# Products that nothing reads, put in front of TensorE's waits in the short stages of the last batch

## The reference

```python
# layer 2, feed-forward ("s5"): activations rounded to 8 bits, ternary weights
h = silu(bit_linear(x, w_gate)) * bit_linear(x, w_up)        # 256 -> 1024
h = rms_norm(h, ln_weight)
x = x + tanh(g) * bit_linear(h, w_down)                      # 1024 -> 256
# layer 3, cross part ("s6"), n = layernorm(x)
attention = softmax((ctx @ Wq.T + bq) @ (ctx @ Wk.T + bk).T)
x = x + tanh(g) * einsum('bln,bmn->blm', n, attention)
# layer 3, feed-forward ("s7"): ternary weights, 256 -> 2048 -> 1024 -> 256
h = silu(gate) * up
x = x + tanh(g) * rms_norm(h) @ wq_p.T
```

## Time and profile before

| what | us |
|---|---|
| median of 3 runs | 1062.55 |
| the profiled execution: its own time | 1062.66 |
| its span in the trace | 1060.9 |
| PE busy (share of the span) | 860.6 (81%) |
| DVE busy | 713.6 (67%) |
| ACT busy | 557.3 (53%) |
| POOL busy | 276.0 (26%) |

### The profile page before, as it was taken

How to read it: one execution, slowest core, us unless ns; L and a number is a source line. 1 busy time by engine, 2 the same in 40 slices (tenths; PEclk the granted TensorE clock), 3 DMA queues, 4 the chain that set the end, 5 groups by cost and what they waited for, 6 DMA issues and landing times.

```text
span 1060.9 us, 13344 instructions
## 1 busy us (share of the span) xinstructions
PE 860.6 (81%) x4116; PEld 616.7 (58%) x4120; DVE 713.6 (67%) x1716; ACT 557.3 (53%) x1318; POOL 276.0 (26%) x365
## 2 busy tenths in 40 slices
PE   3779988755898987798979789979998779699355
PEld 1435655534566865655757567558776656476134
DVE  3896789774548768976889866765568772244643
ACT  8887874222464654446535555653466534466313
POOL 1100212102244201630763113415310423200205
PEclk9999999977999999889999999989999979699568
DMA  7676455445422231341442035404411244111002
GB/s 263 190 249 213 150 170 161 136 161 167 142 90 75 90 105 60 90 125 45 123 151 85 11 114 166 135 25 134 135 61 58 60 126 119 45 31 30 30 1 70
DMA packets 56614, 116.53 MB, mean 110 GB/s; under 512 B 6232, under 2 KB 18400, under 8 KB 55392
## 3 DMA queue, kind: packets, MB, share of 16 engines
q1 hardware_dynamic: 47328, 90.51, 26.8%
q0 software_dynamic: 9216, 25.17, 8.2%
HBM read 97.74 MB, written 17.92 MB: 109 GB/s over the span
## 4 chain that ended last, share of the span: by engine, by line
PE 45%; DVE 22%; issue 16%; POOL 9%; ACT 7%; DMA 1%; POOLq 0%; DVEq 0%; SPq 0%; ACTq 0%
PE bk L1323 29%; PE bk L1402 7%; DVE ssm_u L1948 3%; PE bk L1611 2%; PE bk L1639 2%; DVE ssm_u L1942 2%; POOL aclB L922 1%; PE bk L1387 1%; POOL aclA L922 1%; POOL arA L902 1%; PE bk L1395 1%; DVE mx L2166 1%; POOL arB L928 1%; DVE lnbuf L1853 1%; POOL ring L993 1%
## 5 line engine op out<-in xcount | busy, mean ns | idle before, releaser
L1323 PE MATMUL bk<-hTA,ringT 128*128 128x256 f32 x448 | 109.2, 388 | 1.5 <-DMA ringT<-in_w 1.5
L856 POOL TENSOR_TENSOR lnbuf<-lnbuf,mhalf 128x2 f32<-128x2 f32 x32 | 23.3, 727 | 324.5 <-DVE lnbuf L1859 324.5
L1323 PEld LDWEIGHTS bk<-hTA,ringT 128*128 128x128 f32 x448 | 85.9, 195 | 16.6 <-issue 2.6
L1948 DVE TENSOR_TENSOR_SCAN ssm_u<-ssm_da,ssm_u 128x512 f32<-128x512 f32 x64 | 86.5, 1352 | 4.8 <-ACT ssm_da L1127 1.4
L1323 PE MATMUL bk<-qk 128*128 128x256 f32 x288 | 83.2, 416 | 4.5 <-ACT arB L1209 2.4
L1209 ACT ACTIVATE arB<-bk,nb,rqs 128x256 f32<-128x256 f32 x128 | 70.9, 560 | 24.0 <-DVE nb L2169 23.3
L1323 PE MATMUL bk<-arB,cx 128*128 128x256 f32 x256 | 72.3, 406 | 5.6 <-DVE qk L2205 3.5
L1127 ACT ACTIVATE ssm_da<-sdl,nega 128x255 f32<-128x255 f32 x128 | 57.1, 499 | 35.1 <-DVE ssm_u L1948 34.3
L902 POOL TENSOR_TENSOR arA<-t2A,arA 128x256 f32<-128x256 f32 x44 | 37.1, 844 | 131.6 <-DVE t2A L1981 130.1
L2166 DVE TENSOR_REDUCE mx<-bk 128x2 f32<-128x512 f32 x68 | 46.8, 688 | 32.2 <-PE bk L1323 32.0
L1323 PEld LDWEIGHTS bk<-qk 128*128 128x128 f32 x288 | 56.4, 207 | 19.8 <-issue 8.4
(11 more groups left out here) (339 smaller groups left out, 2172.5 us busy)
## 6 DMA issues: line engine op xcount, KB each, us to landing
ringT<-in_w SPq DMA_DIRECT2D x56, 384.0 KB, 3.4
ringQ<-in_wqk SPq DMA_DIRECT2D x40, 384.0 KB, 3.2
ring<-q3s POOLq DMA_DIRECT2D x32, 384.0 KB, 3.4
ring<-q7s POOLq DMA_DIRECT2D x32, 384.0 KB, 3.5
qk<-kTs SPq DMA_DIRECT2D x32, 256.0 KB, 4.3
ringM<-m4s SPq DMA_DIRECT2D x32, 256.0 KB, 3.3
kTs<-thB SPq DMA_DIRECT2D x11, 256.0 KB, 4.2
kTs<-t1B SPq DMA_DIRECT2D x11, 256.0 KB, 2.0
```

Of the source, the lines that this page charges most:

```text
L1323: return t_.matmul(dst, lhsT, rhs, start=start, stop=stop)
L1948: v.tensor_tensor_scan(row, ssm_da[:, n % 2, :, :].rearrange("p e t -> p (e t)"), row, 0.0, ALU.mult, ALU.add).then_inc(*sig(K, "scan", n))
```

## The change

One new function on TensorE and seven calls of it. `busy(b, n)` does nothing unless b is the last batch; there it waits for `r1.act wT` of that batch (raised long before) and issues n products of the identity with 512 columns of `q5[0]` into `Z0`. No instruction reads what they write. The calls, in the order of the list: 18 ahead of the wait for `hq` (qT of s5), 5 ahead of the wait of the first gu of s5, 14 ahead of each `vq` wait, 10 ahead of the wait of `probsT` of s6, 14 ahead of the transposes of s7, 6 ahead of the wait for `hTl` of the first gu of s7: 81 products. The other engines' lists are the same as before, and so is the order of TensorE's own work.

```diff
+            def busy(b, n):
+                if b == B - 1:
+                    pe.wait_ge(*at(b, "r1.act", "wT"))
+                    for _ in range(n):
+                        mm(Z0[:, :], identb[:, :], q5[0][:, 0:512])
...
@@ swiglu(b, k)
                 yield pl(b, 3)
+                if k == "s7":
+                    busy(b, 14)
                 transpose_h(b, k, hA if k == "s3" else hB, AT if k == "s3" else OP)
...
                     if c == 0:
+                        if k == "s7":
+                            busy(b, 6)
                         pe.wait_ge(*at(b, f"{k}.dve", "hTl"))
@@ s5(b)
                 yield at5(b, AT5["qT"])
+                busy(b, 18)
                 pe.wait_ge(*at(b, "s5.dve", "hq"))
...
                 def down5(t):
+                    busy(b, 14 if t else 14)
                     pe.wait_ge(*at(b, "s5.dve", "vq", t))
...
                     if c == 0:
+                        busy(b, 5)
                         pe.wait_ge(*at(b, "s5.act", "qT"))
@@ s6(b)
                 yield at6(b, AT6["pt"])
+                busy(b, 10)
                 probsT(b, "s6", 0, pm6, OP)
```

## The result

The changed kernel takes 1057.48 us (median of 20 runs, 1054.43 to 1061.52) against 1062.47 (20 runs, 1057.92 to 1067.18): 5.0 us less, ratio 0.9955 with a 95% interval of 0.9943 to 0.9967. The forecast was 1058.9 in a range of 1056.8 to 1062.4. The granted clock, averaged over the whole span, has a median of 0.941 over these 20 runs of the change; over the 35 runs of the kernel before that stand beside e1 to e4 it is 0.924.

What follows compares the result with a forecast made beforehand. In the last batch's tail every engine waits for another, and TensorE steps ending last set the time, many at 1.2 GHz. -0.3 + (0.43 - 0.24) + 0.84 + 0.37 + 1.00 + 1.7 = 3.8; 1062.66 - 3.8 = 1058.9, range 1056.8 to 1062.4.

Steps and rivals of the forecast that it cites:

- The mechanism: Last batch's tail: products in TensorE's waits keep its clock at 2.4 GHz instead of 1.2, so later steps run shorter.
- qT and gu(0): Start of s5: 0.40 us gained if the clock holds behind the 18, 1.28 lost if it falls; 0.3 lost taken.
- vT(1): Behind s5's second vq wait: 0.43 us gained at 2.4 GHz, less 0.24 because the 14 products end late.
- dn(1): End of s5, right ahead of VectorE's residual: 1.89 us at 1.2 GHz against 1.05 at 2.4, 0.84 gained.
- s7's transposes and first gu: Start of s7: at 2.4 GHz instead of 1.2, 0.37 us gained in the transposes and 1.00 in gu(0).
- s6: Stage s6, at 2.4 GHz in the trace but perhaps 1.2 in other executions: 0 to 2.7 us gained, 1.7 taken.
- They shift as a block and keep their length: s7's chunks behind its first gu: clock already 1.00, paced by GpSimd, so they start earlier with no further gain.
- rival 1: Before s5's first gu: the five products become the new wait and s6 gains nothing; 1.1 us gained, 1061.5, chance 0.16.
- rival 2: Before vT(1): the 14 products meet 1.2 GHz and end 4.0 us late; slower, 1064.1, chance 0.09.
- rival 3: Whole tail: the clock falls again in remaining gaps, or the operands don't count as work; 1062.5, chance 0.10.
- The ten in front of probsT: s6's wait of 2.06 us: ten products take 2.20 at 2.4 GHz, costing nothing; 4.3 at 1.2, 2.1 late.

Runs made afterwards that it cites:

- e1: The changed kernel with the same 81 products at 8 columns instead of 512: 1062.03 us, ratio 1.0009 to the kernel before.
- e4: The changed kernel without the 18 and the 5 products: 1057.69 us, ratio 0.9961 to the kernel before.
- e5: The changed kernel with 28 products instead of 14 ahead of the second vq wait: 1061.63 us, ratio 0.9993 to the kernel before.
- e2: The changed kernel with only the 14 and 14 products ahead of the vq waits: 1062.62 us, ratio 0.9989 to the kernel before.
- e6: The changed kernel with only the vq waits' 14 and 14 and s6's 10: 1061.52 us, ratio 0.9988 to the kernel before.
- e9: The changed kernel itself measured once more, on the chip of e10 and e11: 1058.87 us, ratio 0.996 to the kernel before.
- e7: The changed kernel plus products in the waits at the start of the last batch's attention: 1058.24 us, ratio 0.9953 to the kernel before.
- e11: e10 without the attention's products: 1056.85 us, ratio 0.9929 to the kernel before.
- e3: The changed kernel with only s6's 10 and s7's 14 and 6 products: 1059.21 us, ratio 0.9976 to the kernel before.
- e8: e7 with fewer products before the first gu and second vq wait, new ones before dn of s5 and s7: 1056.68 us, ratio 0.9954.
- e10: e7 with 28 for the 18, 3 before each s5 gu, 12 and 12 at vq, others before dn of s5 and s7: 1055.8 us, ratio 0.9931.

## Why the prediction was right, point by point

- **The mechanism**: shown by e1, with the lengths of the steps. With 512 columns a product the mean clock is 0.941 and 5.0 us are gained; with 8 columns and the same instructions it is 0.926, against 0.924 before, and the ratio is 1.0009. Array work in the waits, not instructions, holds the clock, and the clock makes the gain.
- **qT and gu(0), 0.3 lost** as a middle of +0.40 and -1.28: the profiles show +0.42, -0.07, -0.33 and -1.02, and e4 no difference. Right in its bounds; the size can't be told from zero.
- **vT(1), 0.19 gained**: the stretch from the copy of vT(0) to that of vT(1) is 5.85 before and 5.61 after, 0.24. e5 shows that each further product there costs its 0.216.
- **dn(1), 0.84**: 3.01 to 2.16, 0.85.
- **s7's transposes and first gu, 1.37**: 8.18 to 6.96, 1.22. The first gu ran 0.1 longer than the row I took.
- **s6, 1.7 of at most 2.7**: with most of it at 0.50 it took 11.91 (e1) and 11.71 (e2), at 1.00 9.73, so 2.0 to 2.2. In neither was all of it at 0.50 (e1's probsT and e2's scores ran at 1.00), so the 2.7 is neither shown nor excluded. It was right to put a term there, although the trace before showed none; the 1.7 was a guess between bounds, and no run says how often the kernel before meets the one case or the other.
- **"They shift as a block and keep their length"**: this step was short. s7's chunks take 21.36 where the clock comes back early (before, 55.8 behind the start of the attention's last dn) and 22.4 to 22.6 where it does not (e1, e2, e6; 63.1 in e1, 62.5 in e2), and 21.35 to 21.94 in every profile with the 14 and 6. That is a term of 0.6 to 1.2 us that the sum had at nothing, because the one profile before happened to hold the good case.
- **The sum** had 3.8, and 5.0 was measured. With the measured sizes, against e1's profile: 1.0 to 1.5 in s5, 2.2 in s6 (0.6 where the ten are late), 1.2 and 0.6 to 1.2 in s7: 3.5 to 6.1, around the measured 5.0. Against the one profile of the kernel before it would be 2.2, and 0.6 with e9's. So the profiles fit the measured gain only if the kernel before often runs as e1's profile does, which was not counted.
- **Luck**: the range was 5.6 us wide and took in rival 1 at 1061.5 as well, so that it holds the measured time says little. The steps and their lengths say more.
- **Rival 1** occurs (e7's five) and **rival 2** in part (e7's second 14), **rival 3** does not as a whole, since the change is faster by more than its interval, but one thing that it named, a clock that falls again around the scores, occurs in e9 and e11. The ten in front of probsT, which I had at no cost at 1.00 and 2.1 at 0.50, came late in three of the ten profiles that have them: 1.7 in e9, and s6 at 11.35 in e3 and 11.31 in e11.

What stays open is how often each of these happens. One profile stands for one execution, and the runs carry only the mean clock.

## What to carry to other kernels

Where one chain hops between engines, fill TensorE's waits with products up to the wait's length, at the price of a product at the clock that stands there (for 512 columns 0.216 us at 1.00, e5, and 0.43 at 0.50, from e7's five, which took 2.13 until the next product): the last ones past the wait are paid in full (e5, 3.03 for 14). Fill every wait on the way, the short ones too: behind the 18, with 2.60 us left open, the clock held in the change's profile (1.00 from 981.34 to 986.00) and fell in e7's (0.50 from 985.7), where the next filler took 2.34 instead of 1.24. Between vT(1) and the ten, with waits of at most 1.12 us, it held in the change's profile (1.00) and fell in e9's (0.50 from 1018.8). And compare stages between several profiles before a stage is called undisturbed: the single trace before had a tail 3.3 us shorter than that of e1, which takes as long.

## What the runs showed that I had not expected

- The stages up to the last attention's start move by 5.6 us between profiles of kernels that are alike there (905.07 to 910.66), more than the change brings.
- Fourteen products that begin at 0.50 (5.33 instead of 3.19) were free in the change's profile, with 1.96 us until ScalarE is ready for what stands behind them; the same fourteen one step later cost 1.7 (e7).
- The kernel before spends its last attention's start at 0.50 too (909.5 to 929.5). At 1.00 there (e7, e8, e10) that stretch is 66.5 instead of 68.6 to 70.8, but this was not seen in the run times of e7.
